# Normalising x on ScalarE instead of VectorE, with reordered engine programs, in the attention pass of a conditioned transformer kernel

## The reference

```
ada = silu(cond) @ ada_w.T + ada_b          # gamma1, gamma2, scale1, scale2, shift1, shift2
x1  = (x - mean(x)) / sqrt(var(x) + 1e-6) * (scale1 + 1) + shift1
q, k, v = x1 @ mat_qkv_w.T + bias           # 16 heads of 16 channels
q = q / |q| * exp(min(scale_mul, log 100));  k = k / |k|
o = softmax(q k^T) v                        # per sequence and head
x = x + (o @ proj_w.T + proj_b) * gamma1
...                                         # feed-forward, then linear attention
```

## Times and profile before

| | us |
|---|---|
| median of three runs | 1304.96 (1303.32 to 1306.25) |
| the profiled execution | 1303.32, its span 1301.6 |
| first and last statistics of the attention pass | 24.0 and 432.8 |
| last `residual` of the attention pass | 503.8 |
| busy over the whole span: PE, DVE, ACT, POOL | 1165.3, 989.4, 802.9, 845.0 |

### The profile page before, as it was taken

The page is one execution under the profiler, slowest core; times in us unless marked ns, Lnnn a source line. Parts: engine busy times, 40 slices in busy tenths (PEclk is TensorE's granted clock), DMA queues, the critical chain, the costliest instruction groups (busy, mean ns, idle before and its releaser), DMA issues. The chain is left out here.

```text
span 1301.6 us, 37761 instructions
## 1 busy us (share of the span) xinstructions
PE 1165.3 (90%) x12137; PEld 838.6 (64%) x12290; DVE 989.4 (76%) x2338; ACT 802.9 (62%) x2144; POOL 845.0 (65%) x1018
## 2 busy tenths in 40 slices
PE   4687999999999964999999999986999999999996
PEld 3466777777777753566666666663666666666663
DVE  6787999999999836656555556435899999999984
ACT  2676778778877741635454544523676776776764
POOL 4567777777777744546666667542476676676667
PEclk8899999999999986999999999997999999999999
DMA  8542222222222221110101010100011111111112
GB/s 277 143 129 49 56 60 59 59 61 56 58 58 61 62 51 53 26 24 17 33 16 32 16 32 17 33 17 1 17 39 38 40 52 37 40 52 39 44 50 74
DMA packets 138368, 67.73 MB, mean 52 GB/s; under 512 B 76352, under 2 KB 137024, under 8 KB 138304
## 3 DMA queue, kind: packets, MB, share of 16 engines
q1 hardware_dynamic: 109904, 40.92, 12.4%
q10 hardware_dynamic: 28400, 25.99, 6.9%
HBM read 41.18 MB, written 8.65 MB: 38 GB/s over the span
## 5 line engine op out<-in xcount | busy, mean ns | idle before, releaser
L1124 PE MATMUL f_ps_y<-w_fc,f_h_split 128*128 128x256 bf16 x1536 | 172.7, 273 | 2.3 <-DVE f_branch L1243 2.3
L1151 PE MATMUL f_ps_h<-f_x_split,w_fc 128*128 128x512 bf16 x737 | 166.5, 383 | 4.5 <-DVE f_biases L1277 1.4
L1124 PEld LDWEIGHTS f_ps_y<-w_fc,f_h_split 128*128 128x128 bf16 x1536 | 150.2, 98 | 23.6 <-issue 3.0
L657 POOL TENSOR_TENSOR e_split<-e_full,e_split 128x1024 bf16<-128x1024 f32 x64 | 136.6, 2134 | 40.0 <-ACT e_full L730 40.0
L1251 DVE TENSOR_TENSOR f_h_split<-f_h,f_h_split 128x512 bf16<-128x512 f32 x64 | 64.2, 1006 | 104.3 <-ACT f_h L1110 104.3
L1151 PEld LDWEIGHTS f_ps_h<-f_x_split,w_fc 128*128 128x128 bf16 x768 | 75.5, 99 | 89.1 <-issue 3.4
L1109 ACT ACTIVATE f_h_split<-f_ps_h,columns 128x512 bf16<-128x512 f32 x128 | 89.2, 697 | 66.5 <-POOL f_h_split L1066 36.4
L790 PE MATMUL ps_s<-qk_t,k_pairs 128*128 128x64 bf16 x3072 | 102.1, 194 | 29.0 <-DMA k_pairs<-qk_t 25.8
L790 PEld LDWEIGHTS ps_s<-qk_t,k_pairs 128*128 128x128 bf16 x3072 | 97.3, 99 | 37.2 <-issue 19.8
L1066 POOL TENSOR_TENSOR f_h_split<-f_h,f_h_split 128x512 bf16<-128x512 f32 x64 | 79.8, 1257 | 36.7 <-ACT f_h L1110 36.7
L1455 POOL TENSOR_TENSOR l_rstd<-l_mean_var,eps_norm 128x2 f32<-128x2 f32 (+1 forms) x73 | 14.3, 196 | 136.9 <-DVE l_mean_var L1648 107.0
(11 more groups left out here) (187 smaller groups left out, 3233.2 us busy)
## 6 DMA issues: line engine op xcount, KB each, us to landing
v_pairs<-v_split SPq DMA_DIRECT2D x128, 66.0 KB, 2.1
k_pairs<-qk_t SPq DMA_DIRECT2D x256, 32.0 KB, 2.2
gain<-gammas SPq DMA_DIRECT2D x64, 128.0 KB, 3.0
f_gain<-gammas ACTq DMA_DIRECT2D x32, 256.0 KB, 4.3
l_gate<-in_cond ACTq DMA_DIRECT2D x128, 64.0 KB, 2.5
out<-x_all ACTq DMA_DIRECT2D x16, 512.0 KB, 3.0
x_all<-in_x SPq DMA_DIRECT2D x13, 512.0 KB, 5.4
fc_full<-in_L_cond_fc_w SPq DMA_DIRECT2D x2, 1024.0 KB, 7.5
```

Of the source, the lines that this page charges most:

```text
L657: pool.tensor_tensor(flat(e_split[a][:, LO]), flat(e_full[:]), flat(e_split[a][:, HI]), ALU.subtract).then_inc(e_lo_made, 1)
L1124: last = pe.matmul(ps_y[:, i], h_split[a][:, hs, f, i * P:(i + 1) * P], m.w_fc2[:, ws, f], start=(f == 0 and k == 0), stop=(f == F_CHUNKS ...
L1151: last = pe.matmul(ps_h[f % 4][:], m.w_fc1[:, ws, c, f * P:(f + 1) * P], x2_split[a][:, xs, c], start=(k == 0 and c == 0), stop=(k == 2 an ...
```

## The change

x_hat is made on ScalarE as one Identity activation, rstd * x + centre, in place of one tensor_scalar on VectorE. The new operand centre = -mean * rstd takes two more 128x1 products on GpSimd, each behind a semaphore on the one before. rstd is made in the same step as the aggregate, at lag 0 and no longer 1, and x_hat at lag 0, as the last stage of ScalarE's step. TensorE, VectorE, ScalarE, GpSimd and SyncE get another order of stages.

On SyncE the lags of `place_v` and `place_k` go from 5 to 6, and `load_gain` stands at the list's end; since all three act only on every other tile, SyncE's row of issues in the loop is the same cycle of gain, v and k as before. `load_gain` now waits for the buffer's last reader in the loop too. In the written-out steps, the load of `fc2_w` (1024 KB) now stands ahead of the third pair of v and k, not behind it.

```
         def load_gain(t):
...
-                if isinstance(t.n, int):
-                    reuse(sp, branch_made, t, 4)
+                reuse(sp, branch_made, t, 4)
...
-            pipeline(sp, [(9, load_gain), (5, place_v), (5, place_k), (0, load_later)])
+            pipeline(sp, [(6, place_v), (6, place_k), (0, load_later), (9, load_gain)])
...
         def rstd_of(t):
...
                 pool.tensor_tensor(rstd[t.slot(4)][:], rstd[t.slot(4)][:], m.minus_half[:, 0:1], ALU.pow).then_inc(rstd_made, 1)
+                pool.wait_ge(rstd_made, t.n + 1)
+                pool.tensor_tensor(centre[t.slot(4)][:], mean_var[t.slot(4)][:, 0:1], rstd[t.slot(4)][:], ALU.mult
+                                   ).then_inc(mean_scaled, 1)
+                pool.wait_ge(mean_scaled, t.n + 1)
+                pool.tensor_tensor(centre[t.slot(4)][:], centre[t.slot(4)][:], m.minus_one[:], ALU.mult
+                                   ).then_inc(centre_made, 1)
...
-            pipeline(pool, [(5, normalise), (1, rstd_of), (12, add), (2, x1_low), (8, e_lo), (0, split_fc)])
+            pipeline(pool, [(12, add), (0, split_fc), (0, rstd_of), (2, x1_low), (8, e_lo), (4, normalise)])
...
+            def hat(t):
+                a = t.slot(2)
+                act.wait_ge(centre_made, t.n + 1)
+                reuse(act, x_hat_t, t, 2)
+                act.activation(x_hat[a][:, None, :], t.rows(m.x_all), ACT.Identity, bias=centre[t.slot(4)][:],
+                               scale=rstd[t.slot(4)][:]).then_inc(x_hat_made, 1)
...
-            def hat(t):
-                a = t.slot(2)
-                dve.wait_ge(rstd_made, t.n + 1)
-                reuse(dve, x_hat_t, t, 2)
-                dve.tensor_scalar(x_hat[a][:, None, :], t.rows(m.x_all), mean_var[t.slot(4)][:, 0:1], rstd[t.slot(4)][:],
-                                  ALU.subtract, ALU.mult).then_inc(x_hat_made, 1)
...
-            pipeline(dve, [(4, biases), (2, modulate), (4, v_low), (10, outputs), (4, reduce_norms),
-                           (11, residual), (10, o_low), (1, hat), (5, qk_lo), (-1, statistics), (0, aggregate)])
+            pipeline(dve, [(2, modulate), (4, biases), (10, outputs), (-1, statistics), (4, v_low), (0, aggregate),
+                           (4, reduce_norms), (10, o_low), (5, qk_lo), (11, residual)])
```

More of the change, by code:

```diff
@@ L121, in __init__ @@
         self.minus_half = sb("minus_half", [P, UNROLL], F32)
+        self.minus_one = sb("minus_one", [P, 1], F32)
         self.eps_norm3 = sb("eps_norm3", [P, 1], F32)
@@ L301, in _ @@
             pool.memset(m.eps_ln[:], 1e-6).then_inc(consts_made, 1)
+            pool.memset(m.minus_one[:], -1.0)
             pool.memset(m.same_head[:], 1.0).then_inc(consts_made, 1)
@@ L465, in attention_pass @@
         rstd = sb("rstd", [P, 1], F32, 4)
+        centre = sb("centre", [P, 1], F32, 4)
         x_hat = sb("x_hat", [P, C])
@@ L509, in attention_pass @@
         rstd_made = sem("rstd_made")
+        mean_scaled = sem("mean_scaled")
+        centre_made = sem("centre_made")
         x_hat_made = sem("x_hat_made")
@@ L739, in _ @@
             act.preload_act_table_set("natural_log_exp_and_others")
-            pipeline(act, [(4, v_hi), (4, square), (2, modulate_second), (8, high_exponentials), (5, qk_hi),
-                           (10, o_hi), (2, x1_high), (8, full_exponentials), (4, logs), (0, split_fc),
-                           (4, factor)])
+            pipeline(act, [(2, modulate_second), (4, v_hi), (4, square), (2, x1_high), (8, high_exponentials),
+                           (10, o_hi), (4, logs), (5, qk_hi), (8, full_exponentials), (4, factor), (0, split_fc),
+                           (0, hat)])
         @block.tensor
@@ L827, in turn_x @@
                 last.then_inc(x_hat_t, 1)
-            pipeline(pe, [(8, scores), (11, project), (5, turn_qk), (9, probs_v), (10, turn_o), (3, qkv), (1, turn_x)])
+            pipeline(pe, [(8, scores), (9, probs_v), (10, turn_o), (5, turn_qk), (11, project), (1, turn_x),
+                          (3, qkv)])
         @block.vector
```

## The result

The changed kernel takes 1265.51 us (median of 4 runs, 1264.16 to 1269.98), the kernel before 1305.61 beside it: ratio 0.9701, 95% interval 0.9673 to 0.9729. The profiled execution has a span of 1263.1 us against 1301.6. The forecast was 1278, range 1263 to 1299.

The account below looks back on a forecast made before the run. Bound: a three-engine loop of waits (6.82 us), with VectorE's work and the transfers nearly as long. Step 6.75 to 6.2 over 52 steps saves 28.6 us, plus 2 for fc2_w's load: 1276.7 profiled, 1278 forecast, range 1263 to 1299.

Parts of the forecast that it names:

- three-engine loop: Waits through ScalarE, GpSimd and TensorE, from o_hi to the next o_hi: 6.82 us before, 5.8 us after the change.
- loop through the transfers: SyncE's v and k issues, scores, probs_v, next v: nearly as long as the step before, 12.1 us per two steps after.
- VectorE loses `hat`, 0.82 us per step: VectorE's own work per step falls from 6.56 to 5.74 us.
- L839 and the port: VectorE's 128x32 product L839 waits out GpSimd's whole instruction on a shared port: 0.62 us against 0.19.
- the detour: VectorE's way from L839 through ScalarE's logs and qk_hi to qk_lo: 0.94 us, VectorE's loop 5.9 to 6.33.
- ScalarE gains `hat` at 0.41: New activation last in ScalarE's step: 0.41 us from the nearest row, bounds 0.30 and 0.91, its latency covered.
- GpSimd's two products, 0.6 us; floor 5.9: Two added 128x1 products on GpSimd: about 0.6 us per step, between 0.4 and 1.1; its work becomes 5.9.
- 6.2 us per step: Predicted step of the steady stretch, from 6.75; between 6.05 and 6.5, as five loops near 6.0 meet.
- better than that: Whole kernel faster than the forecast case of 1267 to 1286 us; chance 0.04.
- Half of it: Rival: another loop closes at 6.5 us per step, total 1292 us; chance 0.20.
- no change: Rival: v and k transfers hold the step as they do now, total 1305 us; chance 0.06.
- slower: Rival: L839 on VectorE meets GpSimd's e_lo; at 1.4 us held, 7.3 us per step, total 1334; chance 0.08.

Follow-up runs that it names:

- hat_meets: orders_only with x_hat moved to second in VectorE's step, behind modulate, so that it starts after GpSimd's e_lo: 1343.7 us, ratio 1.0300 to the kernel before.
- more_products: The changed kernel with two further 128x1 products per tile on GpSimd, each waited for, result unused: 1277.9 us, ratio 0.9807 to the kernel before.
- sp_old: The changed kernel with SyncE's old list (lags 9, 5, 5, 0): 1266.3 us, ratio 0.9708 to the kernel before.
- dve_old: The changed kernel with VectorE's old order, without x_hat, so the aggregate stands last in its step: 1510.1 us, ratio 1.1558 to the kernel before.
- orders_only: The changed kernel's new orders and lags, but x_hat stays on VectorE, last in its step, without the two products: 1266.7 us, ratio 0.9713 to the kernel before.
- op_only: The kernel before with all its orders, but x_hat made last in ScalarE's step with two products on GpSimd: 1326.1 us, ratio 1.0171.
- op_mid: The kernel before with its orders, but x_hat on ScalarE between qk_hi and o_hi: 1315.7 us, ratio 1.0079.
- turn_first: The changed kernel with one swap on TensorE, turn_qk ahead of probs_v: 1318.0 us, ratio 1.0092 to the kernel before.
- pe_old: The changed kernel with TensorE's old order alone: 1474.7 us, ratio 1.1314 to the kernel before.
- act_old: The changed kernel with ScalarE's old order, x_hat added as its last stage: 1301.7 us, ratio 0.9976 to the kernel before.
- before_swap: The kernel before with two swaps: TensorE runs probs_v and turn_o ahead of turn_qk, ScalarE o_hi ahead of qk_hi: 1286.4 us, ratio 0.9862.

## Why the prediction was right, and where it was not

*What bounds the kernel.* Right in the main: a loop of waits held the step, not VectorE's 93%. Closing the three-engine loop in the new kernel costs 52 us; the swaps that open it in the old one give 18. But the loop through the transfers, which the prediction puts at nearly as long, was closed there as well and is opened by the same swap, so that the three-engine loop alone held the old step isn't shown.

*VectorE loses `hat`, 0.82 us per step.* The row was right and the use of it wrong. I let the removal and the reorder stand as parts of one sum, and the reader could take the operation for half of the gain. By itself it costs 12 to 22 us, and in the new orders it is worth some 0.1 us per step, 4.7 us at the end of the pass, and not to be told from nothing in the total. VectorE needed no relief once L839 and x_hat didn't coincide with GpSimd's work: 0.43 and 0.42 us of its 6.56 were waiting that rows show as busy. (The x_hat at 316.75 ends at 317.66, 0.16 us behind GpSimd's `x1_low` at 316.83 to 317.50, as in hat_meets.)

*L839 and the port.* Right: the hold lasts to the end of the other's instruction (x_hat 1.89 for 0.40), and L839 takes 0.19 now. The 3.633 us of the earlier trace rows is a hold by GpSimd's split of a feed-forward weight (57.35 us, 4.06 long) and not by `e_lo`. I took the end of `add` as its meeting point, so some hold; there is none at 0.192, which takes 0.43 from the detour.

*ScalarE gains `hat` at 0.41.* Mis-sized, though inside its bounds: 0.59. The nearest row was not the copy L678 but the activation L670 with bias and scale from pointers, 0.70 for two of 64 columns. It was covered all the same, in the place it was given.

*GpSimd's two products, 0.6 us; floor 5.9.* About right: 0.27 each from start to start, and 0.62 for the power that they wait for in place of 0.52; the floor by more_products is 5.78.

*6.2 us per step.* The sum's largest term was mis-sized: 6.04. It came out at the transfers' floor of 6.05, whose working (12.1 us for two steps) the rows after confirm with 12.08, and the 0.15 that I added for loops meeting was not needed; TensorE's 6.0 to 6.2 were 5.9. 52 x 0.16 = 8 us of the 12 between forecast and profile. The 2 us for the load of fc2_w can't be told: sp_old, with the load behind the third pair, has its last `residual` 2.8 us earlier in its profile (460.0), but its median is 0.8 us higher. Fill and drain gained 5.7 us together, just over the 5 either way that I left them, and the 2.6 us behind the pass took some of it back.

*The range and the chances.* 1265.5 lies below the 1267 to 1286 to which I gave 0.62. What came is "better than that", with a chance of 0.04; the range of 1263 to 1299 holds it only because it was drawn 4 us wider at that end. So the direction and the bound were foreseen, the size only just.

*The signs.* VectorE at 89%, ScalarE at 93%, GpSimd at 92%, `qk_lo` waiting for qk_t, L839 at 0.19: as said. Not so: VectorE still waits for o_t (5.5 us in 18 of the 33 steps), ScalarE's wait for L839 ahead of `logs` is not among the waits, and `probs_v` follows the scores and not `e_lo`.

*The rivals.* Half of it, no change and slower didn't occur; the slower one's mechanism is real (hat_meets). What the forecast lacked is how steep the landscape is: one engine's list out of step with the others makes the kernel up to 206 us slower than before (dve_old), seven times what I gave the slower case, and by loops that I had not listed.

*What came behind the pass.* I had no term for it. Of the 2.6 us given back, 1.5 lie in the 64 steps of the later pass that ends in `l_mean_var`; first the changed kernel, then orders_only:

```profile
L1659 DVE BATCH_NORM_AGGREGATE l_mean_var<-l_y_stats x64: 171/172/183, 878.9 to 1249.2; 128x2 f32<-128x6 f32 x64
```

```profile
L1659 DVE BATCH_NORM_AGGREGATE l_mean_var<-l_y_stats x64: 170/171/183, 883.6 to 1252.4; 128x2 f32<-128x6 f32 x64
```

From the first to the last it takes 370.3 us in the changed kernel and 368.8 in orders_only, as before the change (368.8). It is 370.2 or more in every kernel that has x_hat on ScalarE (op_only 370.3, op_mid 370.2, turn_first 370.3, pe_old 371.0, act_old 373.0, dve_old 370.2), and 368.7 in before_swap. hat_meets, with x_hat on VectorE, has 369.7, but eight of its steps in the middle take 48.56 us as in orders_only (48.55) and not 48.77 as in the changed kernel; the rest comes in its last steps. The instructions of that pass are the same in all. So the slower steps go with the operation, by a way that stays open, and each figure is from one profile. The whole part behind the attention pass goes less clearly with it: 801.4 us in hat_meets against 800.3 in the changed kernel. In orders_only it takes 797.9, which is why that kernel, 4.7 us behind at the end of the attention pass, is only 2.3 behind in the span.

## What to carry to other kernels

When every engine runs its list in order and several are over 75% busy, follow one round from wait to wait until it closes, and compare its length with the step: that loop, not the busiest engine, can be the bound, and a swap of stages without any change of work can open it. Look for more than one such loop: here two were closed in the old kernel, and one swap opened both. Take an operation off an engine only when that engine's own work is the loop. And change the lists together: three of the four that were put back cost most of the gain or more (SyncE's cost nothing).

## What was not expected of the hardware

In hat_meets, a VectorE operation that comes second to GpSimd's `e_lo` ended 0.15 us behind it, not its own 0.40 (300.21 against 300.06), as if part of it passed before the hold; and when it comes 0.1 us first, as in orders_only, it is GpSimd's instruction that is 0.16 longer (2.29). A held instruction is shown as busy all the while. An Identity activation with scale and bias from SBUF takes 0.59 us at 128x256, a Copy of the same tile size 0.41.
